# Context attention on one Trainium2 core: shifted queries kept in PSUM, value products by single heads on column halves of the array, new cyclic orders

## What is computed

```python
def xattn(x, y):                        # x [16, 64, 512], y [16, 1601, 256]
    q = ln(x @ Wq + bq)                 # per head of 32
    k = ln(y_main @ Wk + bk); v = y_main @ Wv + bv
    s = einsum('bhqd,bhkd->bhqk', q, k) * SCALE
    p = softmax(s)
    ctx = einsum('bhqk,bhkd->bhqd', p, v)
    ctx = ctx + attention_over_last_16_rows
    return ctx @ Wo + bo
```

## Time and profile before

| | |
|---|---|
| median of 3 runs (lowest, highest) | 3159.53 us (3156.69, 3160.48) |
| the profiled execution | 3156.05 us |
| its span | 3154.2 us |
| mean granted TensorE clock | 0.963 |
| busy: PE, PEld | 2869.8 us (91%), 1742.6 us (55%) |
| busy: DVE, ACT, POOL | 2625.1 us (83%), 2282.5 us (72%), 1615.4 us (51%) |

### The profile page before, as it was taken

The page is one execution under the profiler, slowest core; times in us unless marked ns, Lnnn a source line. Parts: engine busy times, 40 slices in busy tenths (PEclk is TensorE's granted clock), DMA queues, the critical chain, the costliest instruction groups (busy, mean ns, idle before and its releaser), DMA issues. The chain is left out here.

```text
span 3154.2 us, 87347 instructions
## 1 busy us (share of the span) xinstructions
PE 2869.8 (91%) x34089; PEld 1742.6 (55%) x34089; DVE 2625.1 (83%) x4082; ACT 2282.5 (72%) x4155; POOL 1615.4 (51%) x2006
## 2 busy tenths in 40 slices
PE   7689999999999878789996779999999999967889
PEld 3245555555555556577773325555555555555546
DVE  6699999999999756768875689999999999957752
ACT  5479999899899855346663459998999999873431
POOL 1257776776777642212223326777767776752210
PEclk9899999999999989889998899999999999988989
DMA  3344544454444344348894435544544444430020
GB/s 127 92 85 88 88 82 86 87 89 81 84 91 79 61 155 146 129 154 297 305 303 137 116 75 88 90 81 87 85 86 85 87 82 86 74 87 10 1 73 27
DMA packets 542690, 328.49 MB, mean 104 GB/s; under 512 B 459381, under 2 KB 504565, under 8 KB 536522
## 3 DMA queue, kind: packets, MB, share of 16 engines
q1 hardware_dynamic: 534314, 295.63, 40.8%
q0 software_dynamic: 7680, 25.17, 2.6%
q10 hardware_dynamic: 288, 2.10, 0.2%
HBM read 181.86 MB, written 36.09 MB: 69 GB/s over the span
## 5 line engine op out<-in xcount | busy, mean ns | idle before, releaser
L334 POOL TENSOR_TENSOR a_elo<-a_e 128x1024 f16<-128x1024 f32 x428 | 858.9, 2007 | 345.3 <-ACT a_e L421 343.4
L590 PE MATMUL a_ps_k<-l_wk,a_yh 128*128 128x512 f16 (+1 forms) x1664 | 571.0, 384 | 33.1 <-POOL a_yl L316 22.6
L590 PE MATMUL a_ps_v<-l_wv,a_yh 128*128 128x512 f16 (+1 forms) x1664 | 568.1, 382 | 11.5 <-DVE a_v L481 10.8
L492 DVE TENSOR_REDUCE a_mx<-a_ps_m 128x2 f32<-128x1024 f32 x384 | 467.3, 1217 | 7.0 <-PE a_ps_m L616 4.8
L419 ACT ACTIVATE a_e<-a_ps_t 128x1024 f32<-128x1024 f32 x428 | 408.9, 955 | 53.3 <-PE a_ps_t L650 51.1
L421 ACT ACTIVATE a_e<-a_ps_t 128x1024 f16<-128x1024 f32 x428 | 409.6, 957 | 0.4 <-PE a_ps_o L678 0.4
L650 PE MATMUL a_ps_t<-a_qb,a_kk 64*128 64x128 f16 (+1 forms) x9672 | 347.8, 218 | 41.3 <-DVE a_qb L516 32.1
L674 PEld LDWEIGHTS a_ps_o<-a_v,a_e 128*128 128x128 f16 (+1 forms) x3240 | 298.5, 96 | 118.4 <-issue 57.2
L674 PE MATMUL a_ps_o<-a_v,a_e 128*128 128x65 f16 (+1 forms) x3240 | 343.9, 193 | 18.4 <-POOL a_elo L334 18.3
L650 PEld LDWEIGHTS a_ps_t<-a_qb,a_kk 64*128 64x128 f16 (+1 forms) x9672 | 276.2, 95 | 128.8 <-issue 67.1
L676 PE MATMUL a_ps_o<-a_v,a_e 128*128 128x64 f16 (+1 forms) x3240 | 342.9, 194 | 0.0
(11 more groups left out here) (423 smaller groups left out, 5944.6 us busy)
## 6 DMA issues: line engine op xcount, KB each, us to landing
l_land<-in_ctx SPq DMA_DIRECT2D x96, 384.0 KB, 3.6
l_ob<-in_m_w SPq DMA_DIRECT2D x32, 1024.0 KB, 13.4
f_w<-in_m_w SPq DMA_DIRECT2D x32, 512.0 KB, 14.2
eo_dram<-f_e_eo SPq DMA_DIRECT2D x32, 512.0 KB, 4.3
l_land<-in_ctx SPq DMA_DIRECT2D x32, 433.0 KB, 3.9
a_kk<-a_khl SPq DMA_TRANSPOSE x416, 3.1
qs_dram<-p_q SPq DMA_DIRECT2D x32, 128.0 KB, 2.4
dca_dram<-p_od SPq DMA_DIRECT2D x16, 256.0 KB, 2.4
```

Of the source, the lines that this page charges most:

```text
L334: pool.tensor_tensor(rest[0:r, :, 0:w], full[0:r, :, 0:w], high[0:r, :, 0:w], ALU.subtract)\
L492: dve.tensor_reduce(mx[:, g, :, c], ps_m[:, :, :], AX.X, ALU.max).then_inc(mx_done, 1)
L590: m = pe.matmul(out[0:r, :], part[:, n % 2, c, cols], w[:, wpart, c, :], start=(c == 0 and a == 0), stop=(c == KC - 1 and a == 2))
```

## The change

- `q1` is no longer a tile in SBUF but the first bank of `ps_m`: `q_shifted` adds in place, `q_high` and `q_low` read it there, and the next batch's first scores wait for `ql_done` where they waited for `q1_done`.
- `v` is laid out by head: 32 high values, a one, 32 low values. A product of values has the 64 queries of one head as weights and that head's 65 (high part of the exponentials) or 33 (rest) columns moving, and writes partitions 0 to 63 for the even head, 64 to 127 for the odd one. A unit has 32 products instead of 24.
- `out` copies the low sums to `ob`, adds the high ones and multiplies by the reciprocal: three instructions on 128 partitions where two on 64 were, with waits between them.
- The four cyclic orders are written anew. They hold the same steps in another sequence. In the old list of PE the kind of product changes between whole array, row halves and `tb` 31 times in a turn; in the new one, with the values as a kind of their own, 46 times.

The diff (of `ORDER` a line of either side of PE and DVE):

```diff
@@ -36,7 +36,7 @@
 TPAIRS = -(-KT // 2)
 UNITS = 2 * TPAIRS
 OW = 65
-VW = 130
+VLO = 33
 CHUNKS = 4
 PER = KT // CHUNKS
 WIDEST = MAIN - (CHUNKS - 1) * PER * P + 1
@@ -49,21 +49,21 @@
 
 
 ORDER = """
...
-    PE: pv10-- m12-- s12-- k6- v5- k7- tb-- s13-- v6- k8- pv11-- v7- pv12-- s0- k9- pv13-- v8- s1- m0- k10-
...
-    DVE: rd7- hat4- ql-- kc8- kl4- vl7- rd8- hat5- kc9- o1-- kl5- vl8- m0- hat6- m1- kc10- kl6- rd9- hat7-
...
+    PE: k2- pv6-- m7-- s8-- v0- k3- pv7-- s9-- m8-- pv8-- v1- k4- s10-- m9-- v2- pv9-- m10-- s11-- k5- m11--
...
+    DVE: qs-- vl4- kc6- kl2- ql-- hat3- vl5- kc7- kl3- rd6- hat4- rd7- kc8- kl4- vl6- hat5- o1-- kc9- kl5-
...
 """
 
 
@@ -107,9 +107,8 @@
         yl = sb("yl", [P, 2, KC, WIDEST], F16)
         khl = sb("khl", [P, 2, 2, D], F16)
         kk = sb("kk", [P, 2, 2 * GROUPS, KCOLS], F16)
-        v = sb("v", [P, 2, KT, PAIRS, VW], F16)
+        v = sb("v", [P, 2, KT, H, OW], F16)
         q0 = sb("q0", [P, 2, GROUPS, S])
-        q1 = sb("q1", [P, GROUPS, S])
         qm = sb("qm", [P, GROUPS, 2, S], F16)
         qb = sb("qb", [P, 2, GROUPS, 2, 2, S], F16)
         e32 = sb("e32", [P, 2, 2, 512])
@@ -150,8 +149,10 @@
         qm_done, sm_done, mx_done, mxx_done = sem("qm_done"), sem("sm_done"), sem("mx_done"), sem("mxx_done")
         tb_done, q1_done, qh_done, ql_done = sem("tb_done"), sem("q1_done"), sem("qh_done"), sem("ql_done")
         s_done, e_done, lo_done, pv_done = sem("s_done"), sem("e_done"), sem("lo_done"), sem("pv_done")
-        rl_done, o_done = sem("rl_done"), sem("o_done")
+        rl_done, os_done, o_done = sem("rl_done"), sem("os_done"), sem("o_done")
         low_done = sem("low_done")
+
+        q1 = ps_m[:, 0, 0:GROUPS * S].rearrange("p (g q) -> p g q", g=GROUPS)
 
         ident, fall, mask, ob = env.ident, env.fall, env.parity_mask[:, :], env.ob
 
@@ -288,7 +289,7 @@
             def _(pool):
                 pool.memset(eps[:, :], HEAD_EPS).then_inc(const_ok, 1)
                 pool.memset(one[:, :], 1.0).then_inc(const_ok, 1)
-                pool.memset(v[:, :, :, :, 64:66], 1.0).then_inc(ones_ok, 1)
+                pool.memset(v[:, :, :, :, HD:VLO], 1.0).then_inc(ones_ok, 1)
                 pool.wait_ge(const_ok, 2)
 
                 def newton_step(at, p):
@@ -396,13 +397,13 @@
                     act.wait_ge(v_done, n + 1)
                     if at.nb >= 2:
                         act.wait_ge(pv_done, 2 + (at.nb - 2) * UNITS + TPAIRS + i // 2 + 1)
-                    act.activation(v[0:r, at.nbp, i, :, 0:64], ps_v[0:r, :].rearrange("p (a d) -> p a d", d=64),
+                    act.activation(v[0:r, at.nbp, i, :, 0:HD], ps_v[0:r, :].rearrange("p (h d) -> p h d", d=HD),
                                    ACT.Copy, scale=1.0 / WSCALE).then_inc(vh_done, 1)
 
                 def q_high(at):
                     act.wait_ge(q1_done, at.nb + 1)
                     for a in range(2):
-                        t = act.activation(qb[:, at.nbp, :, 0, a, :], q1[:, :, :], ACT.Copy, scale=mask[:, a:a + 1])
+                        t = act.activation(qb[:, at.nbp, :, 0, a, :], q1, ACT.Copy, scale=mask[:, a:a + 1])
                     t.then_inc(qh_done, 1)
 
                 def exponent(at, j):
@@ -478,9 +479,9 @@
                 def v_low(at, i):
                     n, r = at.nb * KT + i, rows(i)
                     dve.wait_ge(vh_done, n + 1)
-                    dve.scalar_tensor_tensor(out=v[0:r, at.nbp, i, :, 66:130],
-                                             in0=ps_v[0:r, :].rearrange("p (a d) -> p a d", d=64), scalar=1.0 / WSCALE,
-                                             in1=v[0:r, at.nbp, i, :, 0:64], op0=ALU.mult, op1=ALU.subtract)\
+                    dve.scalar_tensor_tensor(out=v[0:r, at.nbp, i, :, VLO:OW],
+                                             in0=ps_v[0:r, :].rearrange("p (h d) -> p h d", d=HD), scalar=1.0 / WSCALE,
+                                             in1=v[0:r, at.nbp, i, :, 0:HD], op0=ALU.mult, op1=ALU.subtract)\
                        .then_inc(vl_done, 1)
 
                 def maximum(at, m):
@@ -505,15 +506,13 @@
                 def q_shifted(at):
                     dve.wait_ge(tb_done, at.nb + 1)
                     dve.wait_ge(q_in[at.nbp], at.load)
-                    need(dve, ql_done, at.nb)
-                    dve.tensor_tensor(q1[:, :, :], ps_m[:, 0, 0:GROUPS * S].rearrange("p (g q) -> p g q", g=GROUPS),
-                                      q0[:, at.nbp], ALU.add).then_inc(q1_done, 1)
+                    dve.tensor_tensor(q1, q1, q0[:, at.nbp], ALU.add).then_inc(q1_done, 1)
 
                 def q_low(at):
                     dve.wait_ge(q1_done, at.nb + 1)
                     dve.wait_ge(qh_done, at.nb + 1)
                     for a in range(2):
-                        t = dve.scalar_tensor_tensor(out=qb[:, at.nbp, :, 1, a, :], in0=q1[:, :, :], scalar=mask[:, a:a + 1],
+                        t = dve.scalar_tensor_tensor(out=qb[:, at.nbp, :, 1, a, :], in0=q1, scalar=mask[:, a:a + 1],
                                                      in1=qb[:, at.nbp, :, 0, a, :], op0=ALU.mult, op1=ALU.subtract)
                     t.then_inc(ql_done, 1)
 
@@ -522,14 +521,15 @@
                     n = 2 * at.b + half
                     dve.wait_ge(pv_done, at.b * UNITS + TPAIRS * (half + 1) + 2)
                     o3 = ps_o[:, 0:4 * OW].rearrange("p (a d) -> p a d", d=OW)
-                    dve.reciprocal(rl[:, half, :], o3[:, :, 64]).then_inc(rl_done, 1)
+                    dve.reciprocal(rl[:, half, :], o3[:, :, HD]).then_inc(rl_done, 1)
+                    osum = ob[:, at.b, half * P:half * P + P].rearrange("p (a d) -> p a d", d=HD)
+                    dve.tensor_copy(osum, o3[:, :, VLO:OW]).then_inc(os_done, 1)
+                    dve.wait_ge(os_done, 2 * n + 1)
+                    dve.tensor_tensor(osum, o3[:, :, 0:HD], osum, ALU.add).then_inc(os_done, 1)
                     dve.wait_ge(rl_done, n + 1)
-                    for par in range(2):
-                        q = slice(64 * par, 64 * par + 64)
-                        t = dve.tensor_tensor(ob[q, at.b, half * P:half * P + P].rearrange("p (a d) -> p a d", d=HD),
-                                              o3[q, :, HD * par:HD * par + HD],
-                                              rl[q, half, :].unsqueeze(2).broadcast_to([64, 4, HD]), ALU.mult)
-                    t.then_inc(o_done, 1)
+                    dve.wait_ge(os_done, 2 * n + 2)
+                    dve.tensor_tensor(osum, osum, rl[:, half, :].unsqueeze(2).broadcast_to([P, 4, HD]), ALU.mult)\
+                       .then_inc(o_done, 1)
 
                 def low(at, j):
 
@@ -605,7 +605,7 @@
                     wait_turned(pe, at.nb * KT + min(4 * c + 4, KT))
                     if m == 0:
                         pe.wait_ge(qm_done, at.nb + 1)
-                        need(pe, q1_done, at.nb)
+                        need(pe, ql_done, at.nb)
                     need(pe, mx_done, at.nb * MAXES + m)
                     groups = (g,) if m < MAXES - 1 else range(GROUPS)
                     o, w = c * 512, min(512, MAIN - c * 512)
@@ -665,18 +665,19 @@
                     for i in tiles_of(j):
                         k = slice(0, rows(i))
                         for gl in range(2):
-                            col = slice(((i % 2) * 2 + gl) * P, ((i % 2) * 2 + gl + 1) * P)
+                            col = ((i % 2) * 2 + gl) * P
                             for r in range(2):
                                 a = 2 * gl + r
                                 pair = 4 * half + a
                                 first = i == 0 and a == 0
                                 last = i == KT - 1 and a == 3
-                                pe.matmul(ps_o[:, a * OW:a * OW + OW], high[k, r, col], v[k, at.bp, i, pair, 0:OW],
-                                          start=first, stop=False, skip_group_check=True)
-                                pe.matmul(ps_o[:, a * OW:a * OW + 64], high[k, r, col], v[k, at.bp, i, pair, 66:130],
-                                          start=False, stop=False, skip_group_check=True)
-                                t = pe.matmul(ps_o[:, a * OW:a * OW + OW], rest[k, r, col], v[k, at.bp, i, pair, 0:OW],
-                                              start=False, stop=last, skip_group_check=True)
+                                for part, w in ((high, OW), (rest, HD + 1)):
+                                    for par in range(2):
+                                        q = slice(64 * par, 64 * par + 64)
+                                        t = pe.matmul(ps_o[q, a * OW:a * OW + w], part[k, r, col + 64 * par:col + 64 * par + 64],
+                                                      v[k, at.bp, i, 2 * pair + par, 0:w],
+                                                      start=first and part is high, stop=last and part is rest,
+                                                      skip_group_check=True)
```

(25 more changed lines are left out.)

## The result

The changed kernel takes **3082.57 us** (median; 3080.41 to 3084.13) against 3158.11 before (3155.49 to 3160.48): a ratio of **0.9767**, 95% interval 0.9753 to 0.9782, or 75.5 us less. The forecast was 3123, that is 36 us less. The range held the time; the gain is about twice the forecast, and the time is near that of the rival "more is freed" (3087).

A forecast was written before the change was run, and what follows sets the result against it. VectorE was taken as the bound: 58.45 - 1.89 + 0.28 + 1.0 = 57.84 us busy plus 1.35 idle, 59.2 a turn, 1.2 less; times 30, 36 us, so 3120 profiled and 3123 us median, range 3078 to 3188.

The forecast's parts named there:

- more is freed: Rival at the end of `out`: both multiplications find GpSimd idle, a turn 58.0 us, 72 us less, 3087; chance 0.19.
- What bounds the kernel: Context attention turn of 60.4 us: VectorE, busy 58.45 and idle 1.95, taken as the bound, TensorE right behind.
- TensorE idle for more than 1.1 us: Sign in a turn of the changed kernel that would show the forecast right.
- `ql`: VectorE's low query parts: with one SBUF operand, two instructions take 0.66 us in place of 2.55, 1.89 less a turn.
- TensorE: Products of values 0.015 us apart save 3.25 us a turn, changes of kind cost 1.5: 1.75 less.
- I don't book it as time, since VectorE decides: TensorE's 1.75 us less a turn was not counted as time, only as easing the crumbs on VectorE.
- `out`: VectorE's end of a half: 0.97 us, 0.28 more per turn, plus 1.0 a turn waiting for GpSimd (0 to 4.3).
- `o1`: End of one half, directly behind `hat5`: its multiplication should find GpSimd free while ScalarE does `e0`'s exponentials, 1.82 us.
- `o0`: End of the other half: its multiplication has no such shelter from GpSimd, since `lo7` runs about then.
- GpSimd takes it back: Rival at the end of `out`: multiplications wait 1.5 us each, a turn 61.2, 24 us more, 3183; chance 0.18.
- Column halves are dear: Rival on TensorE's products of values: at 0.030 us a record a turn is 62.7, 69 us more, 3228; chance 0.09.
- its second case: Same rival at the skill page's estimate, 0.80 us a unit: 0.9 + 1.5 us more TensorE work, a turn about 61.

The follow-up runs named there:

- s4: The kernel before with three more TensorE products of 512 columns in a turn (0.65 us): 3174.9 us, ratio 1.0065.
- s5: The kernel before with one more VectorE reduction of 128x512 in a turn (0.60 us, spare result, placed behind `ql`): 3157.5 us, ratio 1.0008.
- e5: The kernel before with only the shifted queries moved to PSUM, old orders and old values: 3122.4 us, ratio 0.9894.
- e4: The kernel before with the shifted queries in PSUM and the new orders, values as before: 3118.2 us, ratio 0.9886.
- s1: The changed kernel with one more VectorE instruction of 128x512 in a turn (0.60 us, spare result): 3085.2 us, ratio 0.9777.
- e1: The changed kernel with the four old orders: 3124.9 us, ratio 0.9910 to the kernel before.
- e8: The changed kernel with the four old orders and the reciprocals of `out` in PSUM: 3097.66 us, ratio 0.9825 to the kernel before.

## Why the prediction was wrong

- **What bounds the kernel.** "VectorE's idle time is such crumbs ... it is the engine I take as the bound": this step failed. s4 and s5 show TensorE as the bound before the change: of 19.5 us of spare work on it 19 showed, of 18 us on VectorE 2. The sign "TensorE idle for more than 1.1 us" failed as well: it was idle for 0.15 us of the new turn. The 1.95 us of VectorE against 1.11 of TensorE were on the page; the smaller, and a single wait rather than crumbs, belonged to the engine that I put second.
- **`ql`.** Right in kind and nearly in size: 0.79 us for two, 1.76 less (1.89 taken). But its worth is not VectorE's time: it is the 1.1 us in a turn that TensorE waited for it, 33 us as e5 shows.
- **TensorE.** Products 0.0167 us apart (0.015 taken), a change of kind 0.09 (0.10): both near. With 0.20 us less in a full unit and 0.1 in a half one they give -2.6 + 15 x 0.09 = -1.25 us, where -3.25 + 1.5 = -1.75 was taken; the profile's busy time goes from 59.29 to 57.83 us, 1.46 less. "I don't book it as time, since VectorE decides": these 1.3 us in 30 turns are 39 us, and with the 1.1 us of the wait for `ql` they are the turn's 2.4. The forecast had 1.2. The step from e4 to the changed kernel, V alone under Q and O, is 36 us, near the 39.
- **`out`.** 0.99 us to the successor for 0.97 taken. Its wait for GpSimd, 1.0 us a turn taken, is 0 in this order. This is the term that put the number off: times 30 turns it is 30 of the 40 us between the 3120 forecast for the profiled execution and its 3080. What I had argued for `o1` (GpSimd idle while ScalarE makes `e0`) held; `o0`, which I had left unsheltered, gets ahead of GpSimd by 0.06 us. With this term at 0 the same sum on VectorE gives about 58.2 (VectorE was busy for 56.70 us and idle for 1.28), so it would have come near the time while naming the wrong engine. That nearness would have been luck: s1 and s5 show that 0.6 us of VectorE's work in a turn is not 0.6 us of the turn.
- **The rivals.** "More is freed" had the right number, 58.0, for a reason that was half right: the multiplications do find GpSimd idle, but VectorE's time is not what sets the turn. "GpSimd takes it back" does occur: e1 has 1.36 us of it in a turn, and e8 prices it at 27 us. "Column halves are dear" fell with the 0.0167; its second case, "about 61", adds up to 60.6 by its own terms, and for the "2.2" of idle time and tails in it the rows give only 1.11 of idle time. By the Trainium skill, TensorE: Matmul & The Clock Gate, Back-to-back issue gap, products of up to 64 columns start some 25 ns apart; on two column halves in turn they come at 16.7 on average here. By the Trainium skill, TensorEngine Tiling (Array Packing), Restrictions, column tiling shuts off the fast weight load: here the load of 64 columns is recorded with 113 ns, that of 128 before with 96 to 99, and the products come at 16.7 ns all the same.
- **The numbers.** A share of 0.44 for the forecast and 0.19 for the case that came was the wrong way round. The two differ by the 1.0 us of the wait of `out` and 0.15 us of idle time, so this is that wait's doing. The engine taken as the bound was wrong in both.

## What to carry to other kernels

Where two engines are nearly full, look which one's idle time is a single wait on the other, and test with half a microsecond of spare work on each: the one on which it shows in full is the bound. Put the work at more than one place if a wait lies between. Parts of a change that are worth nothing alone (here the column halves with the old order) may be worth most together, since each only moves the wait to the next place. Before reordering around a VectorE instruction with two SBUF inputs that GpSimd can block, see whether one input can live in PSUM.
